# New orders, lags and banks for the five engines of a two-layer attention kernel, with known waits skipped

## The chip, the cores and the metric

The kernel runs on one core of one Trainium2 chip. A core has five engines that run their own queues of instructions in order: TensorE (PE, matrix products into PSUM), VectorE (DVE), ScalarE (ACT, functions from a table that must be loaded), GpSimd (POOL) and SyncE (SP, which here only issues transfers). They meet at semaphores. The metric is the device time of the program in microseconds (us). The measured kernel of before takes 1125.41 us, the median of 3 runs (1125.07 to 1126.71).

## The reference

64 sequences `x` of 64 tokens with 256 channels, and a context of the same shape. Layer 0 is cross attention, layer 1 a recurrent block (RWKV-like), all in fp32:

```python
h = concatenate([ctx, x]); q = x @ q_w + q_b; k, v = split(h @ kv_w + kv_b)       # 16 heads of 16
attn = softmax(where(mask, q @ k.T / 16, -inf)) @ v @ out_w + out_b + x
x = gelu(rmsnorm(attn) @ mlp_w1 + b1) @ mlp_w2 + b2 + x
xa = ln(x); sx = previous token of xa - xa
xxx = tanh((xa + sx * maa_x) @ maa_w1) @ maa_w2                                   # five mixes
xk, xw, xv, xr, xg = xa + sx * (maa_stack + xxx)
w = exp(-exp(time_decay + tanh(xw @ td_w1) @ td_w2)); r, k, v = xr @ Wr.T, xk @ Wk.T, xv @ Wv.T
g = silu(xg @ Wg.T)
for each token: out = r @ (u * k v + s); s = k v + w * s                          # 32 heads of 8
x1 = x + groupnorm(out) * g @ Wo.T
xc = ln(x1); x = x1 + sigmoid(xr2 @ Wfr.T) * (square(relu(xk2 @ Wfk.T)) @ Wfv.T)
```

## The kernel before

Channels lie on the 128 partitions in two halves; a group is 4 sequences (T = 256 tokens), and 16 groups are worked off. A group's work is cut into named pieces. What sets the order is a string for each engine, `PE_ORDER`, `ACT_ORDER`, `DVE_ORDER`, `POOL_ORDER` and `SP_ORDER` (lines 64 to 75). `turns` (line 86) walks each string once a turn; an entry `2:o` in turn i is piece `o` of group i - 2. The number is the lag. So up to five groups are in work at once, each engine goes through its own list in order, and an engine that waits holds up all that stands behind it. The planning was done outside the kernel; the code has only its result.

PSUM has eight banks. `BANK` (line 60) gives each product its bank, and `tenants` (line 93) works out who had the bank before. `filled[b]` and `freed[b]` count the fillings and readings of bank b: `ready` waits for a product, `taken` until a product was read. `opened` on PE (line 356) waits until the earlier tenant was read. `wait` waits for a value in SBUF.

The pieces of PE, in the order of a group's work: `q`, `k0`, `k1`, `v0`, `v1` (projections from `h_sb`); `sc0`, `sc1` (scores, banks `s0` to `s7`); `tr0` to `tr7` (transposed probabilities); `va0`, `va1`; `o`; `rms`; `w0` to `w3` and `c0` to `c3` (hidden layer up, `psum<-y`, and down, `psum<-hid`); `mean0`, `var0` (first layer norm, `psum<-hsum`); `maa` (`psum<-z`), `xp0`, `xp1`, `x4` (mixes, `psum<-th`); `td1`, `td2`; `K`, `V`, `R`, `G` (`psum<-xm`); `coef`; `ga0`, `ga1` (sums over the state, `psum<-rs`); `cen`, `gvar` (group norm); `O` (`psum<-og`); `mean1`, `var1` (second layer norm); `fk`, `fr` (`psum<-xf`); `fv` (`psum<-xc`, the squared relu).

Between them work, among others: on ACT `ex0` to `ex7` (exponentials of the scores, four instructions each), `pt`, `V`, `K`, `R` (copies from PSUM), `sq`, `lnr`, `lng`, `lna` (squares and inverse roots by Ln and Exp), `sh` (scale and shift), `th`, `tw` (Tanh), `ge0` to `ge3` (Gelu), `e1`, `decay`, `gu`, and the table loads `learnt` (Exp and Ln) and `squashed` (Tanh and Gelu); on DVE `mx` (row maxima), `in` (reciprocals), `y`, `x1`, `hm` and `hv` (sums `hsum` for the norms), `ct`, `nm`, `sx`, `z`, `tm` (`tmp`), `kv`, `st` (the recurrence, as a scan), `bonus`, `sum`, `gn`, `og`, `res`, `xf`; on POOL `pn` (normed probabilities), `xm`, `rk`, `rs` (state times receptance), `act`, `fin`. SP issues `h`, `mask`, `xa`, the small rows `row0` and `row1` (`st_sb`), `s0`, the output `store`, the weights (`load0`, `load1`), and `spread`: eight transfers `vb<-vr` that copy `V` to eight layouts for `kv`.

A matmul in fp32 leaves two records, so four matmuls read as x8.

Of the kernel before, what the change touches and what calls it, by code (L numbers as in the profile page):

```python
# [65 lines left out]
ACT_ORDER = """1:ev1 2:e1 2:decay 0:kt0 1:ysq 1:lna 2:row1 3:relu 2:squashed 2:G 3:tr 1:ge0 1:ge1 1:ge2 1:ge3 0:qt 1:sq0 1:learnt 1:lnr0 1:first 0:vv0 2:gsq 1:sh0
0:kt1 2:lng 0:row0 1:squashed 1:th 2:gu 0:learnt 0:ex1 0:vv1 0:ex0 0:ex2 1:squashed 1:tw 0:learnt 0:ex3 1:V 0:ex4 0:ex5 0:pt1 0:ex6 0:pt3 2:sq1 0:ex7
1:R 0:ev0 1:K 2:lnr1 0:pt5 0:pt7 2:sh1"""
DVE_ORDER = """1:mx3 1:in2 1:mx4 1:mx5 1:in3 1:pt0 1:pt2 1:in4 1:mx6 1:in5 1:mx7 2:tm4 1:in6 3:hv1 1:in7 1:pt4 1:at0 1:pt6 3:nm1 3:sx1 1:fold0 1:at1 3:xf0 2:kv0
2:kv1 2:st0 1:y 0:mask 1:ysum 3:xf1 2:kv2 2:kv3 1:yn 2:kv4 2:st1 2:kv5 2:gate 2:st2 2:kv6 2:st3 2:st4 2:st5 2:st6 2:bonus 1:fold1 2:kv7 1:x1 1:hm0  # L70
2:st7 1:ct0 1:hv0 2:sum 1:fold2 1:nm0 1:sx0 1:z 0:mx0 3:fin 2:gn 0:mx1 2:og 0:mx2 1:tm0 1:tm1 2:res 1:tm2 2:hm1 0:in0 1:tm3 0:in1 2:ct1"""
# [995 lines left out]
```

## Time and profile before

| | us |
|---|---|
| median of 3 runs | 1125.41 |
| the profiled execution | 1126.65 |
| its span, first to last instruction | 1124.9 |
| up to the first `w0` | 48.28 |
| first `w0` to second | 61.19 |
| second `w0` (109.47) to last (1004.69), fourteen turns | 895.22 |
| from the last `w0` on | 120.21 |

| engine | busy, share of the span |
|---|---|
| PE | 1011.7 us, 90% |
| DVE | 761.6 us, 68% |
| ACT | 720.2 us, 64% |
| POOL | 469.5 us, 42% |

The profile is one execution. A row of the view in order of time has the start, the length, the engine, the line of the kernel, the operation, what it writes and reads, and in brackets how long the engine had stood idle and what ended that. Rows whose lengths overlap are pipelined: what a piece costs PE is the distance from its start to the next start.

### The profile page before, as it was taken

Reading aid. Unit: us, or ns where it says so; the run is one execution under the profiler, and the core shown is the slowest. Engines: PE = TensorE matmul, PEld = TensorE weight load, DVE = VectorE, ACT = ScalarE, POOL = GpSimd, SP = SyncE. Lnnn points to the kernel's source line nnn. Section 1 sums busy time; section 2 is a strip of 40 time slices with the busy share of each in tenths; the row PEclk is TensorE's granted clock in tenths of the full one; section 3 lists DMA queues with packets and bytes.
Section 4 is the critical chain, followed back from the end, with each engine's and each line's share of the span. In section 5 each row is a group of like instructions: output and inputs, shape, how many; then the busy total and the mean of one; then the engine's idle time right before and its main releaser. Section 6 shows DMA issues by size and latency. Waiting matters only on the chain.

```text
span 1124.9 us, 20426 instructions
## 1 busy us (share of the span) xinstructions
PE 1011.7 (90%) x6760; PEld 746.6 (66%) x6760; DVE 761.6 (68%) x1275; ACT 720.2 (64%) x2008; POOL 469.5 (42%) x391
## 2 busy tenths in 40 slices
PE   5779999999999999999999999999999999997634
PEld 3566677676867768676867768686777767674412
DVE  2445677676867678686767678686767868685452
ACT  5466584948767594957758494866759494863322
POOL 1114354534435354434435354443535453444240
PEclk9898999999999999999999999999999999998866
DMA  8015060421515051331506042151505133050500
GB/s 293 1 35 76 1 104 8 76 44 45 76 33 87 1 95 26 61 59 45 76 18 103 1 82 38 48 73 44 76 1 104 17 70 51 20 76 10 75 10 9
DMA packets 37127, 61.02 MB, mean 54 GB/s; under 512 B 10464, under 2 KB 13088, under 8 KB 36896
## 3 DMA queue, kind: packets, MB, share of 16 engines
q1 hardware_dynamic: 37024, 59.72, 28.9%
q8 instruction: 56, 0.92, 0.3%
q14 instruction: 47, 0.39, 0.1%
HBM read 21.95 MB, written 4.19 MB: 23 GB/s over the span
## 4 chain that ended last, share of the span: by engine, by line
PE 71%; DVE 8%; SPq 7%; ACT 5%; issue 5%; DMA 3%; POOL 1%; DVEq 0%; POOLq 0%; ACTq 0%
PE psum L366 30%; PE psum L467 10%; SPq L322 6%; PE psum L391 5%; PE psum L384 4%; PE psum L429 4%; PE psum L415 3%; PE psum L498 3%; PE psum L538 3%; DMA st_sb<-stT 3%; PE psum L441 2%; DVE tmp L889 2%; ACT probs L612 2%; PE psum L371 2%; PE psum L548 2%
## 5 line engine op out<-in xcount | busy, mean ns | idle before, releaser
L981 POOL TENSOR_TENSOR rs<-st,rr 128x512 f32<-128x512 f32 x128 | 187.3, 1469 | 303.7 <-DVE st L911 257.0
L911 DVE TENSOR_TENSOR_SCAN st<-decay,kv 128x512 f32<-128x512 f32 x128 | 189.5, 1500 | 20.3 <-POOL rs L981 20.2
L612 ACT ACTIVATE probs<-psum,neg_max 128x128 f32<-128x128 f32 x512 | 183.1, 405 | 1.8 <-DVE neg_max L795 1.4
L956 POOL TENSOR_TENSOR probs<-probs,rsum 128x512 f32<-128x512 f32 x128 | 134.7, 1058 | 59.0 <-DVE rsum L800 59.0
L964 POOL TENSOR_TENSOR xm<-tmp,xs 128x512 f32<-128x512 f32 x80 | 93.6, 1180 | 124.8 <-DVE tmp L889 111.2
L366 PE MATMUL psum<-y,w_sb 128*128 128x256 f32 x512 | 120.2, 389 | 7.5 <-ACT xc L730 3.8
L612 ACT ACTIVATION_READ_ACCUMULATOR probs<-psum,neg_max 128x1 f32 x512 | 125.9, 246 | 0.0
L366 PE MATMUL psum<-xm,w_sb 128*128 128x256 f32 x512 | 124.9, 388 | 0.4 <-POOL xm L964 0.3
L467 PE MATMUL psum<-hid,w_sb 128*128 128x256 f32 x512 | 119.7, 382 | 0.0
L641 ACT ACTIVATE hid<-psum,vec 128x256 f32<-128x256 f32 x128 | 53.7, 471 | 101.5 <-PE psum L366 60.5
L366 PEld LDWEIGHTS psum<-y,w_sb 128*128 128x128 f32 x512 | 98.2, 194 | 26.2 <-DVE y L828 7.2
L467 PEld LDWEIGHTS psum<-hid,w_sb 128*128 128x128 f32 x512 | 96.0, 190 | 25.0 <-issue 12.6
L366 PEld LDWEIGHTS psum<-xm,w_sb 128*128 128x128 f32 x512 | 95.2, 193 | 16.8 <-POOL xm L964 4.5
L795 DVE TENSOR_REDUCE neg_max<-psum 128x4 f32<-128x512 f32 x128 | 85.4, 680 | 23.6 <-PE psum L419 23.6
L593 ACT ACTIVATE qt<-psum,q_bias,vec 128x256 f32<-128x256 f32 x64 | 30.9, 562 | 82.1 <-PE psum L366 82.1
L902 DVE TENSOR_TENSOR kv<-vb,kk 128x504 f32<-128x504 f32 x128 | 83.4, 673 | 0.0
L429 PE MATMUL psum<-mats,probs 128*128 128x128 f32 x512 | 75.6, 284 | 1.7 <-POOL probs L956 1.1
L366 PE MATMUL psum<-xf,w_sb 128*128 128x256 f32 x256 | 66.6, 407 | 11.0 <-DVE xf L747 10.9
L987 POOL TENSOR_TENSOR x<-x,sq 128x512 f32<-128x512 f32 x16 | 20.2, 1265 | 134.3 <-DVE sq L939 134.3
L429 PEld LDWEIGHTS psum<-mats,probs 128*128 128x128 f32 x512 | 59.9, 145 | 15.7 <-issue 5.8
L384 PE MATMUL psum<-h_sb,w_sb 128*128 128x512 f32 x128 | 62.4, 611 | 7.4 <-DMA h_sb<-hT 7.4
L391 PE MATMUL psum<-w_sb,h_sb 128*128 128x256 f32 x256 | 61.8, 384 | 6.1 <-DVE og L926 6.1
(120 smaller groups left out, 1838.2 us busy)
## 6 DMA issues: line engine op xcount, KB each, us to landing
vb<-vr SPq DMA_DIRECT2D x128, 256.0 KB, 7.4
h_sb<-hT SPq DMA_DIRECT2D x16, 512.0 KB, 3.7
xa_sb<-xT SPq DMA_DIRECT2D x16, 256.0 KB, 3.9
out<-x SPq DMA_DIRECT2D x16, 256.0 KB, 2.0
...
```

What stands on the lines that cost most here:

```text
L366: last = mm(to[:, n * T:(n + 1) * T], w(name, k, m * P, m * P + P), rhs[k], start=(k == 0), stop=(k == 1))
L384: last = mm(to, w("k", k, m * P, m * P + P), h_sb[:, k, :, :], start=(k == 0), stop=(k == 1))
L391: last = mm(to[:, i * C:(i + 1) * C], h_sb[:, k, 2 * n + i, :], w("v", k), start=(k == 0), stop=(k == 1))
L429: last = nc.tensor.transpose(to[:, n * P:(n + 1) * P], probs[:, u % PROBS, n, :], mat("ident"))
L467: last = mm(to[:, m * T:(m + 1) * T], w2_sb[:, 2 * n + i, m * P:(m + 1) * P], hid[:, n % 2, i, :], start=(n == 0 and i == 0 and m == 0), s ...
L612: last = fn(probs[:, u % PROBS, n, :], bank(g, f"s{u}")[:, n * P:(n + 1) * P], ACT.Exp, bias=neg_max[:, u % PROBS, n:n + 1], accum_out=sum ...
L795: nc.vector.tensor_reduce(neg_max[:, u % PROBS, :], bank(g, f"s{u}").rearrange("p (n k) -> p n k", n=4), AX.X, ALU.max, negate=True).then_ ...
L902: tt(kv[:, j, :, 1:S], batches(vb[:, j, :])[:, :, 0:S - 1], batches(flat(kk))[:, :, 0:S - 1], ALU.mult).then_inc(kv_made.sem, 1)
L911: nc.vector.tensor_tensor_scan(st[:, n % 2, :], decay[:, :, :, :].rearrange("p h b s -> p (h b s)"), kv[:, j, :, :].rearrange("p b s -> p ...
L956: tt(probs[:, u % PROBS, :, :], probs[:, u % PROBS, :, :], rsum[:, u % PROBS, :].unsqueeze(2).broadcast_to([P, 4, KEYS]), ALU.mult).then_i ...
L964: tt(xm[:, k % XM, :, :].rearrange("p h (b s) -> p (h b) s", b=GB), tmp[:, k % TMP, :, :].rearrange("p h (b s) -> p (h b) s", b=GB), xs[0] ...
L981: tt(rs[:, (RH * g + n) % RS, :], st[:, n % 2, :], flat(rr), ALU.mult).then_inc(rs_made.sem, 1)
```

## The change

Every order string, the lags in them and the banks are replaced. The pieces of DVE, POOL and SP stay the same and move. On PE too, with lags 0 to 3 for 0 to 4. ACT gets one more `learnt` and one more `squashed` a turn, eight loads for six. `reach` now remembers for each engine the highest value it has waited for on a semaphore and leaves a wait out that this already covers. And the bank wait (`opened`) stands ahead of the wait for the data in every piece of PE.

```diff
@@ -57,20 +57,20 @@
-BANK = {"q": 4, "k0": 3, "k1": 6, "v0": 1, "v1": 4, "bias": 1, "s0": 5, "s1": 2, "s2": 0, "s3": 1, "t0": 4, "t1": 7, "t2": 0, "t3": 4, "a0": 4, "s4":
...
+BANK = {"q": 4, "k0": 5, "k1": 7, "v0": 4, "v1": 0, "bias": 3, "s0": 3, "s1": 1, "s2": 6, "s3": 0, "t0": 2, "t1": 0, "t2": 5, "t3": 4, "a0": 6, "s4":
...
-SP_ORDER = """2:xa 1:row0 1:load0 3:spread 3:row1 4:store 1:load1 0:h 1:s0 0:mask"""
...
+SP_ORDER = """2:load1 3:spread 4:store 1:load0 1:row0 1:xa 0:h 1:s0 2:row1 0:mask"""
...
@@ -271,22 +271,29 @@
+        known = {}
+
+        def reach(eng, name, sem, value):
+
+            if value > known.get((id(eng), name), 0):
+                known[id(eng), name] = value
+                eng.wait_ge(sem, value)
+
         def ready(eng, g, name):
 
             if g >= 0:
                 b, n = USE[g, name]
-                eng.wait_ge(filled[b], n + 1)
+                reach(eng, ("filled", b), filled[b], n + 1)
...
         def wait(eng, event, g, k):
 
-            if g * event.n + k > 0:
-                eng.wait_ge(event.sem, g * event.n + k)
+            reach(eng, event.name, event.sem, g * event.n + k)
...
-            def average(g, name, src):
-
-                return mm(opened(g, name)[:, 0:T], mat("mean256"), src[:, :], start=True, stop=True)
+            def average(g, name, src, made):
+
+                to = opened(g, name)
+                wait(pe, made, g, 1)
+                return mm(to[:, 0:T], mat("mean256"), src[:, :], start=True, stop=True)
...
-                    for name in ("q", "k0", "k1"):
+                    for name in ("k0", "q", "k1"):
...
                 elif piece in ("K", "V", "R", "G"):
                     n = "KVRG".index(piece) + 1
+                    to = opened(g, piece)
                     wait(pe, xm_made, g, n + 1)
```

What moves on PE between the end of the hidden layer and the mixes, before (`c3`, `q`, `fv`, `mean0`, `v0`, `ga1`, `var0`, `cen`, `k1`, `gvar`, `sc0`, `maa`):

```order
L467 MATMUL psum<-hid,w_sb 128x256 x4
L366 MATMUL psum<-h_sb,w_sb 128x256 x4
L366 MATMUL psum<-xc,w_sb 128x256 x4
L371 MATMUL psum<-hsum,mats 128x256
L391 MATMUL psum<-w_sb,h_sb 128x256 x4
L538 MATMUL psum<-rs,heads 32x512 x4
L371 MATMUL psum<-hsum,mats 128x256
L548 MATMUL psum<-gt,center 128x512
L384 MATMUL psum<-h_sb,w_sb 128x512 x2
L551 MATMUL psum<-kk,same 128x512
L415 MATMUL psum<-kt,qt 128x128 x16
```

The same place on PE after (`c2` and `c3`, `fk`, `mean0`, `coef`, `ga1`, `var0`, `fr`, `tr0`, `cen`, `fv`, `maa`):

```order
L476 MATMUL psum<-hid,w_sb 128x256 x8
L373 MATMUL psum<-xf,w_sb 128x256 x4
L380 MATMUL psum<-hsum,mats 128x256
L552 MATMUL psum<-z,bonus_w 128x256 x2
L546 MATMUL psum<-rs,heads 32x512 x4
L380 MATMUL psum<-hsum,mats 128x256
L373 MATMUL psum<-xf,w_sb 128x256 x4
L437 MATMUL psum<-mats,probs 128x128 x4
L557 MATMUL psum<-gt,center 128x512
L373 MATMUL psum<-xc,w_sb 128x256 x4
L492 MATMUL psum<-z,w_sb 128x256 x2
```

One product instead of two stands between `c3` and `mean0`, and more work than before between `ga1` and `cen`.

DVE from the recurrence up to `x1` (`L911` and `L924` are the scans `st`), before:

```order
L902 TENSOR_TENSOR kv<-vb,kk 128x8x63
L911 SCALAR_TENSOR_TENSOR st<-decay,kv 128x512
L902 TENSOR_TENSOR kv<-vb,kk 128x8x63
L894 SCALAR_TENSOR_TENSOR gate<-gt,psum 128x512
L911 SCALAR_TENSOR_TENSOR st<-decay,kv 128x512
L902 TENSOR_TENSOR kv<-vb,kk 128x8x63
L911 SCALAR_TENSOR_TENSOR st<-decay,kv 128x512 x4
L917 TENSOR_TENSOR gt<-psum,vr 128x512
L902 TENSOR_TENSOR kv<-vb,kk 128x8x63
L833 SCALAR_TENSOR_TENSOR x<-psum,vec,xa_sb 128x256 x2
L840 TENSOR_TENSOR hsum<-x 128x256
L911 SCALAR_TENSOR_TENSOR st<-decay,kv 128x512
```

DVE after, up to the same instruction:

```order
L924 SCALAR_TENSOR_TENSOR st<-decay,kv 128x512 x2
L808 TENSOR_REDUCE neg_max<-psum 128x4 x3
L915 TENSOR_TENSOR kv<-vb,kk 128x8x63 x2
L760 SCALAR_TENSOR_TENSOR xf<-sx,vec,xs 128x256 x2
L924 SCALAR_TENSOR_TENSOR st<-decay,kv 128x512
L760 SCALAR_TENSOR_TENSOR xf<-sx,vec,xs 128x256 x2
L924 SCALAR_TENSOR_TENSOR st<-decay,kv 128x512
L915 TENSOR_TENSOR kv<-vb,kk 128x8x63
L813 RECIPROCAL rsum<-sums 128x4
L907 SCALAR_TENSOR_TENSOR gate<-gt,psum 128x512
L924 SCALAR_TENSOR_TENSOR st<-decay,kv 128x512
L808 TENSOR_REDUCE neg_max<-psum 128x4
```

Behind these comes the last scan and then `x1`. All eight scans now stand ahead of `x1`, with four row maxima and both `xf` among them; before, the eighth followed `hm0`.

ACT around `tw`, after (before, a softmax tile stood ahead of `tw`, and `gu` and `lng` further up):

```order
L595 ACT_TABLE_LOAD
L585 ACTIVATE kk<-psum,vec 128x512
L587 ACTIVATE kk<-kk 128x512
L597 ACT_TABLE_LOAD
L695 ACTIVATE tw<-psum 128x128
L619 ACTIVATE vv<-psum 128x512
L595 ACT_TABLE_LOAD
L625 ACTIVATE probs,sums<-psum,neg_max 128x128 x4
L591 ACTIVATE vr<-psum 128x512
L738 ACTIVATE og<-og,gnv 128x256 x2
```

The load ahead of the group norm's root (`kk`) is the added `learnt`.

## Rows read from the trace of the kernel before

**Rows 1.** Busy time by stretch: us, then each engine, clock, DMA share, GB/s
```profile
0.00:48.28 48.28, 28.49 (x223) 20.05 (x223) 14.67 (x39) 25.52 (x87) 8.77 (x15) 0.89 0.49 171
48.28:109.47 61.19, 53.10 (x367) 41.01 (x367) 28.09 (x70) 36.90 (x111) 16.40 (x15) 0.92 0.31 51
493.05:556.58 63.53, 61.41 (x424) 45.67 (x423) 47.59 (x79) 44.24 (x126) 29.40 (x24) 1.00 0.30 54
1004.69:1124.90 120.21, 70.50 (x276) 46.42 (x276) 58.62 (x79) 38.83 (x62) 37.71 (x27) 0.78 0.14 25
```

**Rows 2.** PE in order of time, one steady turn: start, us, instruction, [idle before]
```profile
506.33 1.99 PE L467 MATMUL psum<-hid,w_sb 128*128 128x256 f32 x8
508.16 1.89 PE L366 MATMUL psum<-h_sb,w_sb 128*128 128x256 f32 x8
...
511.62 0.59 PE L371 MATMUL psum<-hsum,mats 128*128 128x256 f32 x2
...
514.86 0.70 PE L371 MATMUL psum<-hsum,mats 128*128 128x256 f32 x2
515.82 1.13 PE L548 MATMUL psum<-gt,center 128*128 128x512 f32 x2 [0.26 <-DVE gt L921]
...
519.76 1.17 PE L415 MATMUL psum<-kt,qt 32*128 32x128 f32 x32 [0.24 <-issue]
...
523.13 1.96 PE L391 MATMUL psum<-w_sb,h_sb 128*128 128x256 f32 x8 [0.47 <-DVE og L926]
...
530.51 0.70 PE L371 MATMUL psum<-hsum,mats 128*128 128x256 f32 x2 [0.78 <-DVE hsum L840]
531.55 1.17 PE L415 MATMUL psum<-kt,qt 32*128 32x128 f32 x32 [0.35 <-DVE tmp L889]
```

**Rows 3.** DVE in order of time; then one POOL row; then one page group
```profile
508.43 0.88 DVE L833 SCALAR_TENSOR_TENSOR x<-psum,vec,xa_sb 128x256 f32<-128x256 f32 x2 [1.37 <-PE psum L467]
509.41 1.28 DVE L840 TENSOR_TENSOR hsum<-x 128x256 f32<-128x256 f32 x1
...
519.56 0.88 DVE L747 SCALAR_TENSOR_TENSOR z<-sx,vec,xs 128x256 f32<-128x256 f32 x2
...
530.04 0.41 DVE L840 TENSOR_TENSOR hsum<-x 128x256 f32<-128x256 f32 x1
...
551.66 0.85 DVE L820 SCALAR_TENSOR_TENSOR y<-psum,o_bias,xa_sb 128x256 f32<-128x256 f32 x2
...
509.15 1.26 POOL L981 TENSOR_TENSOR rs<-st,rr 128x512 f32<-128x512 f32 x1
...
L795 DVE TENSOR_REDUCE neg_max<-psum 128x4 f32<-128x512 f32 x128 | 85.4, 680 | 23.6 <-PE psum L419 23.6
```

**Rows 4.** ACT in order of time, the same turn
```profile
523.23 1.08 ACT L725 ACTIVATE og<-og,gnv 128x256 f32<-128x256 f32 x2
...
532.01 1.28 ACT L582 ACT_TABLE_LOAD   x1
533.30 0.37 ACT L612 ACTIVATE probs<-psum,neg_max 128x128 f32<-128x128 f32 x1
...
544.69 1.06 ACT L578 ACTIVATE probs_t<-psum 128x512 f32<-128x512 f32 x2
...
548.20 0.83 ACT L687 ACTIVATE decay<-psum,vec 128x252 f32<-128x252 f32 x2
549.06 0.62 ACT L693 ACTIVATE decay<-decay 128x504 f32<-128x504 f32 x1
```

**Rows 5.** Waits: total, times, longest; then PE, DVE, ACT rows near the end
```profile
ACT xs L654 <- DMA st_sb<-stT: 13.6, 6, 8.4
...
1044.02 3.72 PE L366 MATMUL psum<-xm,w_sb 128*128 128x256 f32 x16 [0.34 <-POOL xm L964]
...
1069.41 0.69 DVE L894 SCALAR_TENSOR_TENSOR gate<-gt,psum 128x512 f32<-128x512 f32 x1 [2.96 <-ACT gt L713]
...
1105.20 1.28 ACT L572 ACT_TABLE_LOAD   x1 [1.89 <-PE psum L371]
```

More of the change, by code:

```diff
@@ L57 @@
 LEARNT, SQUASHED = "natural_log_exp_and_others", "gelu_apprx_tanh_and_others"
-BANK = {"q": 4, "k0": 3, "k1": 6, "v0": 1, "v1": 4, "bias": 1, "s0": 5, "s1": 2, "s2": 0, "s3": 1, "t0": 4, "t1": 7, "t2": 0, "t3": 4, "a0": 4, "s4":
[3 rows of a table removed]
-PE_ORDER = """2:o 3:G 4:fk 2:rms 4:fr 2:w0 2:w1 2:w2 2:c0 2:c1 2:w3 2:c2 3:ga0 2:c3 1:q 4:fv 2:mean0 1:v0 3:ga1 2:var0 3:cen 1:k1 3:gvar 1:sc0 2:maa 1:v1 2:xp0 3:O
-2:xp1 2:td1 3:mean1 1:sc1 2:V 1:tr0 1:tr1 1:tr2 2:K 1:tr3 1:bias 2:x4 1:tr4 2:R 1:va0 3:var1 1:tr5 1:tr6 1:tr7 0:k0 1:va1 2:td2 2:coef"""
@@ L66 @@
[L66 to L69, printed above, removed]
@@ new lines @@
+PE_ORDER = """1:tr3 1:tr2 2:K 3:O 2:x4 2:td2 1:va0 3:mean1 1:tr5 2:R 1:tr6 3:var1 1:tr4 1:tr7 0:q 1:va1 0:k0 1:o 0:k1 0:v0 1:rms 2:G 0:sc0 1:w0 1:w1 1:c0 1:w2 1:c1
+2:ga0 1:w3 1:c2 1:c3 3:fk 1:mean0 2:coef 2:ga1 0:bias 1:var0 3:fr 0:tr0 2:cen 3:fv 1:maa 2:gvar 1:xp0 1:xp1 0:v1 1:td1 0:sc1 1:V 0:tr1"""
+ACT_ORDER = """4:relu 2:sq0 2:lnr0 3:row1 2:sh0 3:gsq 4:squashed 4:tr 2:th 3:learnt 3:lng 2:squashed 2:tw 1:vv1 1:learnt 1:ex4 2:V 3:gu 1:ex5 1:pt1 1:pt3 2:K 1:ex6
+2:e1 1:ex7 3:sq1 1:ev0 2:decay 1:pt5 2:R 3:lnr1 1:pt7 1:ev1 0:qt 1:ysq 0:kt1 0:kt0 3:sh1 1:lna 0:vv0 1:squashed 1:ge0 2:G 1:ge1 0:learnt 0:ex0 0:ex2
@@ new lines @@
+1:squashed 1:ge2 1:row0 1:ge3 0:learnt 0:ex3 1:first 0:ex1"""
+DVE_ORDER = """1:mx7 1:pt2 3:res 3:hm1 1:in5 2:tm4 3:ct1 1:in6 1:in7 3:hv1 1:at0 1:pt6 1:pt4 3:nm1 2:kv0 2:kv1 1:at1 2:kv2 2:st0 2:st1 1:y 1:ysum 2:kv3 2:kv4 0:mask
+3:sx1 1:yn 2:st2 2:st3 0:mx0 0:mx1 0:mx2 2:kv5 2:kv6 3:xf0 2:st4 3:xf1 2:st5 1:fold1 2:kv7 0:in0 2:gate 1:fold2 2:st6 0:mx3 2:st7 1:x1 1:hm0 0:fold0
+1:ct0 2:bonus 1:hv0 2:sum 1:nm0 0:in1 0:pt0 1:sx0 1:z 3:fin 1:tm0 1:tm1 1:tm2 0:in2 0:in3 1:tm3 2:gn 0:mx4 0:mx5 0:in4 0:mx6 2:og"""
@@ L378, in piece_of @@
                 if piece == "q":
-                    project(opened(g, "q"), "q", [h_sb[:, k, :, S:KEYS] for k in range(HALVES)]).then_inc(filled_by(g, "q"), 1)
+                    project(to, "q", [h_sb[:, k, :, S:KEYS] for k in range(HALVES)]).then_inc(filled_by(g, "q"), 1)
                 elif piece in ("k0", "k1"):
                     m = int(piece[1])
-                    to = opened(g, piece)
                     for k in range(HALVES):
@@ L387, in piece_of @@
                     n = int(piece[1])
-                    to = opened(g, piece)
                     for i in range(2):
@@ L446, in piece_of @@
                         pe.wait_ge(ld_w[1].sem, 16)
+                    to = opened(g, "o")
                     for bp in range(2):
                         taken(pe, g, f"a{bp}")
-                    project(opened(g, "o"), "o", [attn[:, :, k, :] for k in range(HALVES)]).then_inc(filled_by(g, "o"), 1)
+                    project(to, "o", [attn[:, :, k, :] for k in range(HALVES)]).then_inc(filled_by(g, "o"), 1)
                 elif piece == "rms":
-                    wait(pe, ysum_made, g, 1)
-                    average(g, "rms", ysum).then_inc(filled_by(g, "rms"), 1)
+                    average(g, "rms", ysum, ysum_made).then_inc(filled_by(g, "rms"), 1)
                 elif piece in ("w0", "w1", "w2", "w3"):
@@ L456, in piece_of @@
                         pe.wait_ge(folded.sem, 4)
+                    to = opened(g, piece)
                     wait(pe, normed, g, 1)
-                    project(opened(g, piece), "w1", [y[:, k, :] for k in range(HALVES)], (2 * n, 2 * n + 1)).then_inc(filled_by(g, piece), 1)
+                    project(to, "w1", [y[:, k, :] for k in range(HALVES)], (2 * n, 2 * n + 1)).then_inc(filled_by(g, piece), 1)
                 elif piece in ("c0", "c1", "c2", "c3"):
@@ L481, in piece_of @@
                         pe.wait_ge(ld_small.sem, 80)
+                    to = opened(g, "maa")
                     wait(pe, z_made, g, 1)
-                    to = opened(g, "maa")
                     for k in range(HALVES):
@@ L491, in piece_of @@
                     pair = (0, 1) if piece == "xp0" else (2, 3)
+                    to = [opened(g, f"x{n}") for n in pair]
                     taken(pe, g, "maa")
-                    to = [opened(g, f"x{n}") for n in pair]
                     for m in range(HALVES):
@@ L517, in piece_of @@
                 elif piece == "td2":
+                    opened(g, "td2")
                     taken(pe, g, "td1")
-                    opened(g, "td2")
                     to = wide(g, "td2")
@@ L540, in piece_of @@
                 elif piece == "coef":
+                    to = opened(g, "coef")
                     wait(pe, rk_made, g, 1)
-                    to = opened(g, "coef")
                     for m in range(HALVES):
```

46 lines of the change are left out of this document (24 added, 22 removed), and 6 rows, old and new, of the table BANK.

## The prediction

> **What bounds the kernel now.** I read first the table of busy times by stretch [rows 1], cut where TensorE (PE) starts the first hidden-layer product `w0` of a group. Up to the first `w0` it takes 48.28 us, to the second 61.19, to the last one (1004.69) fourteen more turns, and 120.21 us are left then. The fourteen turns make 1004.69 - 109.47 = 895.22, 63.94 each. In the turn shown PE is busy 61.41 of 63.53 us at clock 1.00; VectorE (DVE) 47.59, ScalarE (ACT) 44.24, GpSimd (POOL) 29.40. So PE sets the turn, and only three things can give time: the 2.1 us in which it stands, the turns that are longer than this one, and the ends, where PE is busy 28.49 of 48.28 and 70.50 of 120.21 us.
>
> Second, PE in order of time [rows 2]. The idle time stands in brackets: 0.26 before the centering `cen`, 0.24 before the scores `sc0`, 0.47 before `v1`, 0.78 before `mean1`, 0.35 before `sc1`: 2.10 together, and these same five return in nearly every turn. 63.53 - 2.10 = 61.43 is the turn of this work with no wait in it.
>
> Third, who makes turns longer [rows 5]: ACT waited six times, 13.6 us in all, for the 4 KB load `st_sb`, once for 8.4. That is the load `row1`, which SP issues behind the eight `vb` transfers. The mean turn is 0.4 above the one shown.
>
> **The change, part by part.** Work per group is the same on PE, DVE and POOL: only orders, lags and banks move. ACT gets two more table loads a turn, eight for six.
>
> *Old waits.* `cen` gets `var0`, `fr` and `tr0` between itself and `ga1` (before only `var0`): gone. `sc0` waited for nothing but its eight semaphores; they are now four or five, the known ones being skipped: I take 0.1 left. `v1` opened a bank that `cen` held until DVE read it, and now takes bank 0 from `maa`, read by ACT before `xp0`: gone. `mean1` gets `x4`, `td2` and `va0` behind `O`, some 2.3 us against a chain of two DVE instructions: gone. `sc1` stood for `tmp`; it now stands 4.6 us behind the start of `xp0`, the third `tmp` is ready at some 4.4: gone, but close. The row load is issued before the spread of the next group and has most of a turn to land: the 0.4 goes.
>
> *New waits.* A product of four matmuls over 256 columns takes 1.73 (3.46 for `q` and `fv`, from 508.16 to 511.62) [rows 2]. Before, these two covered what lies between `c3` and `mean0`; now only `fk` does, 1.73. The chain there: `x1` 0.88, `hm0`, and about 0.1 for each hand-over. `hm0` took 1.28 where POOL worked beside it (POOL 509.15 for 1.26) and 0.41 where it did not [rows 3]. So `mean0` could follow `c3` by 1.5 or 2.4, and PE waits nothing or 0.7. POOL's `rs7` now starts as `x1` does, so nearer to the second. Also DVE can come late to `x1`. From `y` (551.66, or 488.1 a turn earlier) to where it stood ready for `x1` (508.43 - 1.37 idle = 507.1) it took 19.0. In that stretch the change puts `sx1`, four `mx`, the first `xf` and one reciprocal, takes out one `kv`, `bonus` and a wait of 1.3 for POOL: with 0.68 a `mx` [rows 3] some +1.6, plus about 1.2 in which it now waits for `ysq` and the root. With `y` starting 1.0 behind `o` that makes 22.8 from the end of `o`, against 22.2 of PE work (eight `w` and `c`, `k1`, `v0`, `G` at 1.73 make 19.0; `sc0`, `rms`, `ga0` and changes of shape 3.2). 0.6 late at most; I take 0.8 for `mean0` in all, 0 and 1.6 being the ends.
>
> `mean0` to `var0`: the chain `ct0`, `sq0`, `hv0` takes 2.7; the cover is `mean0`, `coef`, `ga1`, 2.4: 0.3. `var0` to `maa`: from 514.86 to the end of `z` (519.56 + 0.88) are 5.6 [rows 2, 3], the cover `var0`, `fr`, `tr0`, `cen`, `fv` makes 5.5: 0.1. For the many other hand-overs that now stand within half a microsecond (`K`, `td2`, `q`, `tr3`, `O`) I take 0.2 together, with 0.1 of `sc0` 0.3. New turn: 61.4 + 0.8 + 0.3 + 0.1 + 0.3 = 62.9.
>
> *ACT.* The longest run without rest is now from `tw` to `pt7`, before `va1` may start. The same run before went from the load at 532.01 to 545.75: 13.74. The change adds `gu` 1.08, `e1` 0.83 and `decay` 0.62 to it and takes one softmax tile, 1.4 (four instructions, spaced 0.35), out [rows 4]: 14.9. It starts 5.4 behind `xp0`, so `pt7` is done at 20.3; PE comes to `va1` 21.1 behind `xp0` by the same kind of count. Slack 0.8: no wait, but this is the place where the new order is tightest. Of the two added loads one stands before `lng`, the other beside the hidden layer (`learnt` and `squashed` around `ex0`, `ex2`), where ACT waits for PE. I cost both at nothing; uncovered they cost 1.28 each.
>
> A load takes 1.28, and the next instruction starts 0.01 behind it (532.01 + 1.28 = 533.29, then 533.30) [rows 4]. The Trainium skill, page "ScalarE: Activation LUTs", section "What ACT_TABLE_LOAD costs", gives 1283 ns for the load, as here, and a drain of 1380 ns more at every switch to another set; that page asks to group work by set, which speaks against eight loads. By the rows two loads more are 2.6 us of ACT a turn, by the page 5.3. It is the slower rival below.
>
> *First turns.* The order opens with `q`, `k0`, `k1`, `v0` and `sc0` of group 0, and now puts five pieces of group 1 before the first `w0`, into idle time. The softmax of group 0 still sets that point: 48.3, 47 to 53. The load of the later weights is issued behind `h` of group 1, some 20 us later, yet first needed after 48. To the second `w0` I count 57 instead of 61.2: 61.4 less `O`, `mean1`, `var1`, `ga0`, `gvar` of groups that do not exist yet and less part of the ACT run; the third is 62.
>
> *The end.* From the last `w0` to `V` of that group (1044.02) it took 39.3 [rows 5]. In the new order some 33: the hidden layer and `ga0` 14.9 with their changes of shape, then 2.5, 2.7, 5.7 by the chains above, 2.5 from `maa` to `xp0` and 4.6 to `V`. -6. Then DVE stood 2.96 for `gt`, because ACT stood 8.4 for the row [rows 5]: -3. The last `lnr1` (1105.20) loads two tables on the chain, since no `learnt` piece is left there; now one stands ahead of `lng` in the same turn: -1.3 there and two of 1.28 at `lnr1`: -3.9. Against these, `kv0` of the last group waits a little longer behind `nm1`, and scans and POOL hold each other up as before: I take back 3. 120.2 - 10 = 110, from 106 to 116.
>
> **Sum.** 48.3 + 57 + 62 + 13 x 62.9 + 110 = 1095.0 for the span. The profiled execution took 1126.65 at a span of 1124.9, 1.75 more, and the median of the runs is 1125.41, 1.24 below it: 1095.0 + 1.75 - 1.24 = 1095.5, say 1096.
>
> **Rivals.**
> *A, forecast*, turn 62.9: 1096.
> *B, all covered.* `hm0` takes 0.41, DVE is in time, PE waits 0.3: turn 61.8, 1096 - 13 x 1.1 = 1082. For it: each new wait was rounded up. Against: `rs7` beside `hm0`.
> *C, a turn no shorter than the one shown.* DVE comes 1.5 or more late to `x1`, or two of the near hand-overs fall on the other side; turn 63.7 to 64.2, 13 x 1.0 more: 1109, faster by the ends alone. For it: DVE and POOL slow each other by amounts that depend on how they meet.
> *D, slower: the ACT run is the bound.* Between `maa` and `K` it now holds three table loads. If each costs as long again as its row, 3 x 1.3 = 3.9, less the slack of 0.8, PE waits 3.1 a turn more: 1096 + 13 x 3.1 = 1136. It decides against the change from 29 / 13 = 2.3 us a turn on, when the run is 3.1 longer than I count. Against it: the 0.01 behind every load in [rows 4]. The page's rule on the drain is this case; the trace does not bear it out.
> *E, nothing to be seen* from skipped waits and banks, and gains at the ends given back in the turns: 1125.
>
> **Numbers.** A 0.50, B 0.13, C 0.24, D 0.09, E 0.04. Predicted is A, 1096. The range takes in B and C and the width of the ends: 1078 to 1117. A measurement of this kernel tells 0.2%, 2.3 us, from no change. Faster 0.87, same 0.03, slower 0.10.
>
> **What would show it.** Turns from `w0` to `w0` of 62.9; the five old waits gone; in their place `mean0` waiting for `hsum` by under 1 us and `var0` by some 0.3; ACT never waiting for `st_sb`; `va1` not waiting for ACT; the last `w0` near 985 and 110 us behind it; no pair of table loads in the last `lnr1`. The forecast is wrong if the turn is above 64, or if PE waits for ACT at `K`, `va1` or `q` in each turn.

## The result, and the profile after

The changed kernel takes 1078.15 us (median of 4 runs, 1072.45 to 1079.97), the kernel before, on the same chip, 1126.06 (4 runs, 1125.07 to 1127.48): ratio 0.957, interval 0.955 to 0.959. The forecast was 1096 with a range of 1078 to 1117. The direction was right and the size was not: 48 us gained where 29 were forecast.

Busy time by stretch, the changed kernel, cut again at the starts of the first, second and third `w0`, around one steady turn and at the last `w0`; the answer to [rows 1]. Columns: stretch, us, then PE, PEld, DVE, ACT, POOL, clock, DMA share, GB/s.

```profile
0.00:54.57 54.57, 37.33 (x279) 26.91 (x279) 14.96 (x37) 29.40 (x93) 8.78 (x15) 0.87 0.48 152
54.57:114.68 60.11, 51.53 (x366) 39.19 (x362) 32.55 (x73) 39.47 (x113) 18.71 (x16) 0.89 0.32 52
...
479.09:539.61 60.52, 59.41 (x426) 44.96 (x422) 46.15 (x79) 46.73 (x127) 31.27 (x24) 1.00 0.32 56
...
962.62:1076.80 114.18, 68.38 (x297) 48.16 (x295) 60.05 (x81) 41.50 (x66) 37.53 (x26) 0.81 0.15 26
```

The third stretch, to 176.43, is 61.75. So the first `w0` stands at 54.6 (48.3 forecast), the next two stretches are 60.1 and 61.75 (57, 62), thirteen turns average (962.62 - 176.43) / 13 = 60.48 (62.9), and the end is 114.2 (110). The turns were forecast 31.5 us too long in all, the ends and the second stretch 13.6 too short. The turn is where the miss is. It lost 2.00 us of busy PE (61.41 to 59.41), where the prediction had it unchanged, and stands for 1.1 us in place of 2.1.

PE in the same turn in order of time, the answer to [rows 2]; idle time before a row in brackets.

```profile
494.20 1.89 PE L373 MATMUL psum<-xf,w_sb 128*128 128x256 f32 x8
496.09 0.67 PE L380 MATMUL psum<-hsum,mats 128*128 128x256 f32 x2
...
498.90 0.67 PE L380 MATMUL psum<-hsum,mats 128*128 128x256 f32 x2 [0.28 <-DVE hsum L866]
...
501.57 1.02 PE L557 MATMUL psum<-gt,center 128*128 128x512 f32 x2
...
506.96 1.16 PE L505 MATMUL psum<-th,maa_sb 32*128 32x256 f32 x16
508.05 1.99 PE L399 MATMUL psum<-w_sb,h_sb 128*128 128x256 f32 x8
510.44 0.66 PE L522 MATMUL psum<-xm,w_sb 128*64 128x128 f32 x8 [0.40 <-POOL xm L977]
511.36 1.17 PE L423 MATMUL psum<-kt,qt 32*128 32x128 f32 x32 [0.25 <-DVE tmp L902]
...
512.82 1.97 PE L373 MATMUL psum<-xm,w_sb 128*128 128x256 f32 x8 [0.17 <-POOL xm L977]
```

The waits ahead of `cen`, `v1` and `mean1` are gone and that of `sc0` does not show. `mean0` (496.09) follows `fk` with no idle time shown; the only new wait that the prediction named and that shows is `var0`'s 0.28. `td1` 0.40, `sc1` 0.25 and `V` 0.17 wait behind `xp0`/`xp1`. The sixteen products of `xp0` and `xp1` now make one group of 1.16 us, and `v1` starts 1.09 behind them. This is the main thing that the prediction missed.

DVE in the same turn, the answer to [rows 3], and then the scans as a group of the page.

```profile
477.88 2.33 DVE L924 TENSOR_TENSOR_SCAN st<-decay,kv 128x512 f32<-128x512 f32 x2
...
494.40 0.88 DVE L846 SCALAR_TENSOR_TENSOR x<-psum,vec,xa_sb 128x256 f32<-128x256 f32 x2 [1.03 <-PE psum L476]
495.31 0.64 DVE L853 TENSOR_TENSOR hsum<-x 128x256 f32<-128x256 f32 x1
...
L924 DVE TENSOR_TENSOR_SCAN st<-decay,kv 128x512 f32<-128x512 f32 x128 | 163.6, 1301 | 0.5 <-POOL rs L994 0.5
```

DVE is not late to `x1`: it stands 1.03 us for PE. `hm0` took 0.64, between the 0.41 and 1.28 of [rows 3]. A scan takes 1301 ns on average, as against 1500 before.

ACT, the answer to [rows 4]: three loads of 1.28 (one ahead of `kk`, one on either side of `tw`), then the last transposed tile and the wait behind it.

```profile
506.58 1.28 ACT L595 ACT_TABLE_LOAD   x1
...
509.24 1.28 ACT L597 ACT_TABLE_LOAD   x1
511.15 0.28 ACT L695 ACTIVATE tw<-psum 128x128 f32<-128x128 f32 x1 [0.62 <-PE psum L522]
...
511.93 1.28 ACT L595 ACT_TABLE_LOAD   x1
...
526.52 0.60 ACT L591 ACTIVATE probs_t<-psum 128x512 f32<-128x512 f32 x1
529.36 0.48 ACT L636 ACTIVATE o_even<-psum,vec 128x256 f32<-128x256 f32 x1 [2.23 <-PE psum L449]
```

`pt7` ends at 527.12, 20.2 behind `xp0`; PE starts `va1` at 528.15, 21.2 behind it. The prediction had 20.3 and 21.1. This count was right.

The end, the answer to [rows 5]: ACT of the last two groups, with the loads that stand on its way, then PE at `V` of the last group.

```profile
981.42 1.28 ACT L585 ACT_TABLE_LOAD   x1
983.29 1.28 ACT L587 ACT_TABLE_LOAD   x1
...
1010.47 1.28 ACT L585 ACT_TABLE_LOAD   x1
1012.26 1.28 ACT L587 ACT_TABLE_LOAD   x1
...
1059.88 0.47 ACT L585 ACTIVATE r_rs<-psum,vec 128x256 f32<-128x256 f32 x1 [1.77 <-PE psum L380]
...
997.26 3.32 PE L373 MATMUL psum<-xm,w_sb 128*128 128x256 f32 x7 [1.70 <-POOL xm L977]
```

The wait for `st_sb` is gone, and the last `lnr1` (1059.88) has no load. But the code issues the pieces `learnt` and `squashed` only for groups that exist, so now the two `lnr` before it have two loads each on their way, at 981 and at 1010. `V` of the last group starts 34.6 behind the last `w0` (33 forecast).

### The profile page after: what moved, and what is told of

Read it like the earlier page. It is cut to its first block, busy times and chain, and to the rows that moved or that the text cites. A ratio compares the mean times of both kernels' runs of the same rounds, so it can differ in the third digit from the quotient of the medians.

```text
span 1076.8 us, 18987 instructions
## 1 busy us (share of the span) xinstructions
PE 979.2 (91%) x6760; PEld 735.7 (68%) x6760; DVE 753.3 (70%) x1275; ACT 762.3 (71%) x2040; POOL 500.2 (46%) x391
## 4 chain that ended last, share of the span: by engine, by line
PE 80%; DVE 6%; ACT 5%; POOL 5%; issue 4%; DMA 0%; POOLq 0%; DVEq 0%; SPq 0%; ACTq 0%
PE psum L373 36%; PE psum L476 10%; PE psum L393 5%; PE psum L437 5%; PE psum L380 4%; POOL xm L977 4%; PE psum L399 3%; PE psum L449 3%; PE psum L492 2%; PE psum L423 2%; PE psum L505 2%; PE psum L546 1%; PE psum L561 1%; ACT probs L625 1%; PE psum L552 1%
## 5 line engine op out<-in xcount | busy, mean ns | idle before, releaser
L994 POOL TENSOR_TENSOR rs<-st,rr 128x512 f32<-128x512 f32 x128 | 206.5, 1629 | 226.6 <-DVE st L924 196.7
L969 POOL TENSOR_TENSOR probs<-probs,rsum 128x512 f32<-128x512 f32 x128 | 146.7, 1157 | 181.6 <-DVE rsum L813 181.6
L924 DVE TENSOR_TENSOR_SCAN st<-decay,kv 128x512 f32<-128x512 f32 x128 | 163.6, 1301 | 0.5 <-POOL rs L994 0.5
L625 ACT ACTIVATION_READ_ACCUMULATOR probs<-psum,neg_max 128x1 f32 x512 | 116.5, 228 | 0.0
L373 PEld LDWEIGHTS psum<-y,w_sb 128*128 128x128 f32 x512 | 94.8, 190 | 27.4 <-issue 15.8
L915 DVE TENSOR_TENSOR kv<-vb,kk 128x504 f32<-128x504 f32 x128 | 96.3, 781 | 0.0
L902 DVE SCALAR_TENSOR_TENSOR tmp<-psum,vec,sx 128x256 f32<-128x256 f32 x128 | 54.6, 479 | 53.8 <-PE psum L505 42.8
L808 DVE TENSOR_REDUCE neg_max<-psum 128x4 f32<-128x512 f32 x128 | 82.2, 675 | 13.4 <-PE psum L427 13.4
L595 ACT ACT_TABLE_LOAD x64 | 82.1, 1283 | 1.1
L597 ACT ACT_TABLE_LOAD x64 | 82.1, 1283 | 1.1
L437 PE MATMUL psum<-mats,probs 128*128 128x128 f32 x512 | 71.3, 279 | 2.5 <-POOL probs L969 1.3
L399 PE MATMUL psum<-w_sb,h_sb 128*128 128x256 f32 x256 | 65.7, 402 | 2.1 <-ACT probs L625 2.1
```

Source lines behind the costliest of these rows:

```text
L373: last = mm(to[:, n * T:(n + 1) * T], w(name, k, m * P, m * P + P), rhs[k], start=(k == 0), stop=(k == 1))
L399: last = mm(to[:, i * C:(i + 1) * C], h_sb[:, k, 2 * n + i, :], w("v", k), start=(k == 0), stop=(k == 1))
L437: last = nc.tensor.transpose(to[:, n * P:(n + 1) * P], probs[:, u % PROBS, n, :], mat("ident"))
L595: sc.preload_act_table_set(LEARNT)
L625: last = fn(probs[:, u % PROBS, n, :], bank(g, f"s{u}")[:, n * P:(n + 1) * P], ACT.Exp, bias=neg_max[:, u % PROBS, n:n + 1], accum_out=sum ...
L808: nc.vector.tensor_reduce(neg_max[:, u % PROBS, :], bank(g, f"s{u}").rearrange("p (n k) -> p n k", n=4), AX.X, ALU.max, negate=True).then_ ...
```

## The experiments

All are one edit to one of the two kernels. "Turn" is the median from `w0` to `w0` in the profiled execution, between the third `w0` and the fifteenth; medians of times are of several runs. Against the changed kernel only the turns tell small differences: its own runs lie between 1072.45 and 1079.97. The "fill" is the stretch up to the first `w0`, the "end" that from the last one on.

**1. `v1` between `xp0` and `xp1`.**

```
-2:gvar 1:xp0 1:xp1 0:v1 1:td1
+2:gvar 1:xp0 0:v1 1:xp1 1:td1
```

> The changed kernel with xp1 moved behind v1, nothing else. In the changed kernel xp0 and xp1 together take 1.09 us of TensorE, before each took 1.06. Theory 1: the four mixes use four different 32-row strips of the array, and their products run beside each other only when they are adjacent in the queue. Then both take 1.06 again here, TensorE is busy 1.0 longer in a turn, and the waits of 0.40, 0.26 and 0.17 behind them mostly go, because they only stand there since the mixes are early: turn 60.5 to 60.8, the time 1078 to 1083. Theory 2: the 1.09 is an artefact of missing or modelled records; then the start distances from xp0 to td1 stay and the turn stays 60.5.

Measured: 1089.61 us (1082.54 to 1092.77). The turn is 61.24, PE busy 60.38. The rows on PE:

```profile
505.03 1.13 PE L505 MATMUL psum<-th,maa_sb 32*128 32x256 f32 x8
506.09 1.99 PE L399 MATMUL psum<-w_sb,h_sb 128*128 128x256 f32 x8
508.02 1.13 PE L505 MATMUL psum<-th,maa_sb 32*128 32x256 f32 x8
509.08 0.66 PE L522 MATMUL psum<-xm,w_sb 128*64 128x128 f32 x8
```

Here `td1` (509.08) waits for nothing. Each half takes 1.06 when it stands alone and both together take 1.09: the four strips of 32 rows run beside each other. Standing together saves 0.97 of busy time a turn; 0.25 of it goes back into waits. Net 0.72, 13 turns of which are 9.4 us. So the first theory had the cause right, and turn and time came out above what it expected, since fewer waits went away than it took.

**2. Every wait issued again.**

```
-            if value > known.get((id(eng), name), 0):
-                known[id(eng), name] = value
+            if value > 0:
                 eng.wait_ge(sem, value)
```

> The changed kernel with every wait issued again, known or not (1912 waits on TensorE for 1321), orders, lags and banks as changed. Theory A: a wait that is already met costs TensorE about 0.05 us where pieces are short, so the transposes take 0.50 instead of 0.44 each and the turn grows by 0.6 to 1.0 us, the time by 10 to 16. Theory B: met waits are passed ahead of time and cost nothing except in front of the scores (0.24 once a turn): turn grows by 0.1 to 0.3, the time by 2 to 5.

Measured: 1085.44 (1084.84 to 1091.08), turn 60.87, PE busy 59.58. PE issues 1912 waits in the program in place of 1321, 37 more a group, and a turn is 0.35 longer, half of it in PE's busy time and half in its waits. Neither number expected (0.6 to 1.0, or 0.1 to 0.3) held. Shared out over PE's 37, that is some 0.01 us for a wait already met, as an estimate, for the edit brings waits back on the other engines too. The end is 118.7 in this execution for 114.2; what makes it longer stays open.

**3. The new code with the old tables of orders and banks.**

```
-BANK = {...}  PE_ORDER ... SP_ORDER of the changed kernel
+BANK = {...}  PE_ORDER ... SP_ORDER of the kernel before
```

> The kernel before in orders, lags and banks, with the new code: known waits skipped (1354 for 1831 on TensorE) and bank waits first. Theory A: 0.6 to 1.0 us a turn less, 1110 to 1116. Theory B: 0.1 to 0.3 less, 1121 to 1125, and all else of the gain is in the tables.

Measured: 1119.68 (1116.17 to 1127.3), turn 63.38, PE busy 61.12. The median lies between the two expectations, nearer to B. The ratio to before is 0.996 (0.994 to 0.999). So of the 48 us the code (known waits skipped, bank waits first) gives some 6 by the medians, 1 to 7 by the interval, and the tables 41. The turn of before was 63.70 in the median: 0.3 from the code, 2.9 from the tables.

**4. Data waited for first, banks after** (the body of the TensorE block of before, with the new tables and skipped waits; one of some twenty such places).

```
-                    to = opened(g, piece)
                     wait(pe, normed, g, 1)
-                    project(to, "w1", ...
+                    project(opened(g, piece), "w1", ...
```

> The changed kernel with the waits of each piece of TensorE in the old order (data first, bank second), known waits still skipped. Both theories: bank waits are nearly always met, so which stands first matters little: 1078 to 1080. A theory by which bank waits first is worth something (the last wait in the queue is the one that is late) gives 0.05 at each of the four places that wait, 0.2 a turn, 1081.

Measured: 1072.97 (1068.48 to 1077.55), turn 60.33, where `var0` waits 0.19 in place of 0.28. In the new order "bank waits first" costs 0.19 a turn, 2.5 us in all; the times alone do not show it, they lie within the scatter of the changed kernel.

**5. The row load `row1` of before, issued ahead of `spread`.**

```
-SP_ORDER = """2:xa 1:row0 1:load0 3:spread 3:row1 4:store ...
+SP_ORDER = """2:xa 1:row0 1:load0 3:row1 3:spread 4:store ...
```

> The kernel before with one edit: on SP's queue the store that fills scratch rows for the second norm stands ahead of the transfer that spreads gamma, instead of behind it. Theory: in before, three of 15 turns ran 3 to 6 us late only because ScalarE or SP's queue waited there, and part of the end's 110 us is the same wait; with the order exchanged no turn is longer than 64.2 and the time falls by 4 to 9 us, to 1116 to 1121. Rival: the time is set by TensorE's own instructions and the five waits, so nothing moves: 1124 to 1127.

Measured: 1122.22 (1117.43 to 1125.99), ratio to before 0.997 (0.9945 to 0.9991). ScalarE waits for `st_sb` nowhere in it. In the kernel before, four of the six such waits reached PE: `w0` opens the bank of `fk`, and ScalarE's `relu`, which reads it, stands behind `row1`. First ScalarE and PE in order of time, then PE's line in the view of waits (total, times, longest), all of the kernel before:

```profile
237.22 0.21 ACT L654 ACTIVATE xs<-st_sb 128x8 f32<-128x8 f32 x1 [1.65 <-DMA st_sb<-stT]
...
238.06 4.12 PE L366 MATMUL psum<-y,w_sb 128*128 128x256 f32 x18 [1.68 <-ACT xc L730]
...
PE psum L366 <- ACT xc L730: 3.8, 4, 1.7
```

These 3.8 us are gone. From the second `w0` to the last it takes 893.1 in place of 895.2, so 2.2 less: this execution has two turns of 65.06 where the other has one of 65.05. In such a turn PE is busy 62.94 and not 61.4, and the granted clock is at the lower level for 3.4 us; the stretch in the kernel before, in the columns of [rows 1]:

```profile
723.70:727.10 3.40, 3.40 (x40) 2.72 (x38) 2.34 (x6) 3.03 (x10) 3.40 (x4) 0.50 0.00 0
```

Why the clock fell in these turns and not in others, which have the same waits ahead of that point, stays open. 4.0 more are in the end (116.1 for 120.2), where the wait of 8.4 us is gone, and 1.6 are lost again between the first `w0` and the second. So the theory was right on the waits, and wrong that no turn would be longer than 64.2.

**6. The first `v1` in bank 7.**

```
-            bank = BANK[name]
+            bank = 7 if (g, name) == (0, "v1") else BANK[name]
```

> The changed kernel with the very first v1 (group 0) put in bank 7 in place of bank 0, where it waited for the scores of the first group to be read (2.09 us on ScalarE's probs) before 16 matmuls at half clock. Theory that this wait is on the path of the fill: first w0 starts 2 us earlier (52.5 where the changed kernel had 54.6) and the time is 1075 to 1077. Rival, that the fill is set by ScalarE's own work: first w0 stays at 54 to 55 and the time at 1078 to 1079.

Measured: 1071.83 (1071.08 to 1073.95), first `w0` at 50.13, the next stretch 58.1. The fill's PE rows, first of the changed kernel, then of this one:

```profile
25.07 3.78 PE L399 MATMUL psum<-w_sb,h_sb 128*128 128x256 f32 x8 [2.09 <-ACT probs L625]
```

```profile
22.66 3.57 PE L399 MATMUL psum<-w_sb,h_sb 128*128 128x256 f32 x8
27.20 1.17 PE L423 MATMUL psum<-kt,qt 32*128 32x128 f32 x32 [0.97 <-DVE probs_t L818]
```

The wait of 2.09 is gone and half of it comes back ahead of `sc1`, now for DVE. In both, `v1` takes about twice its 1.89 us; PE had been idle for most of the 5 us ahead (busy 1.65 between 20 and 25 in the changed kernel), and the granted clock of the changed kernel between 25 and 30 us is 0.50, the lower level (1.2 GHz). The first `w0` came 4.4 us sooner than in the profiled execution of the changed kernel, more than the 2 expected. Most of that is no effect of the edit: a second execution without it, in the next experiment, has 50.94.

**7. The same table asked for twice more.**

```
-1:vv1 1:learnt 1:ex4
+1:vv1 1:learnt 1:learnt 1:learnt 1:ex4
```

> The changed kernel with two more table loads in each turn, right behind the learnt one that stands ahead of ex4 (ten loads a turn in place of eight). A traced load takes 1.28 us, so 2.57 us more of ScalarE a turn; the last transposed probabilities are ready 1.0 us ahead of va1. Theory A (a load costs its 1.28 us and nothing else, slack 1.0): turn 60.5 to 61.5 or 62.0, time 1093 to 1102. Rival B (each switch also costs a drain of 1.38 us that the row does not show): turn + 4.3, time 1140 to 1150. Rival C (ScalarE has more slack there than the last wait shows): turn below 60.9, time under 1085.

Measured: 1074.87 (1072.41 to 1079.06), turn 60.53, and still 64 rows of loads for each of the two pieces: the added requests for a table that is already in left no row and took no time. Whether the chip passes over them or they never reach it, the run does not show, and it says nothing on ScalarE's slack. It is of use as a second execution of the changed kernel: its first `w0` stands at 50.94 where the one above has 54.57, its third stretch is 60.30 for 61.75, its turns are equal to 0.01 us. By the third `w0` the two executions stand 6.6 us apart (176.43, 169.87), by which products of the fill meet the lower clock: `k0` and `k1` of group 0 took 4.66 us there and 3.60 here, three tiles of probabilities 2.79 and 2.17, the second `q` 3.35 and 1.89. A single profiled execution tells the fill to some 4 us and a steady turn to 0.01. Over the ten executions that have the new tables the first `w0` stands between 50.1 and 54.6, over the four with the old ones between 48.3 and 48.8.

**8. Table loads kept in the last two turns.**

```
-            if 0 <= i - lag < GROUPS and ...
+            if (0 <= i - lag < GROUPS or piece in ("learnt", "squashed") and GROUPS <= i - lag and i <= GROUPS + 1) and ...
```

> The changed kernel with the table loads named learnt and squashed also issued in the two turns behind the last group, where the changed kernel leaves them out because the group that they belong to does not exist. Without them six loads of the end stand exposed in front of the work that needs them (two in front of each of the pairs at 981 and 1010 us, one at 1045 and one hidden at 1069). Theory: each load taken off the chain that ends last gives 1.28 us, three to four of them are on it: 1073 to 1075, the stretch from the last w0 to the end 109 to 110 in place of 114.2. Rival: the end is set by TensorE's recurrence and VectorE, the loads only moved the idle time: 1077 to 1079, stretch 113 to 114.

Measured: 1074.24 (1069.1 to 1074.93). ScalarE at the end:

```profile
974.29 0.63 ACT L662 ACTIVATE sq<-xc 128x512 f32<-128x512 f32 x1 [0.62 <-DVE xc L861]
976.32 0.47 ACT L585 ACTIVATE r_rs<-psum,vec 128x256 f32<-128x256 f32 x1 [1.40 <-PE psum L380]
...
1000.70 0.63 ACT L662 ACTIVATE sq<-xc 128x512 f32<-128x512 f32 x1 [0.75 <-DVE xc L861]
...
1004.77 1.09 ACT L684 ACTIVATE xs<-xc,vec 128x256 f32<-128x256 f32 x2 [1.21 <-DVE xc L870]
```

No load stands between `sq` and the `lnr` behind it (976.32), and from the second `sq` to the `xs` two steps behind (1000.70 to 1004.77) it is 4.1 us, where it was 6.3 (1008.46 to 1014.79). The end is 111.2 long, against 114.2 and 114.4 in the two executions without the edit: 3.1 us, 2.4 loads' worth, where three to four were expected.

**9. A maximum between two scans.**

```
-2:st2 2:st3 0:mx0
+2:st2 0:mx0 2:st3
```

> The changed kernel with one maximum (mx0) put between the scans st2 and st3 on VectorE, which stand next to each other in it. In the changed kernel two scans that stand together take 2.33 us; in the kernel before single ones took 1.70 us each, beside work of GpSimd. Theory A (a scan is short because another scan follows it): the two now take 1.5 to 1.7 each, VectorE is busy 0.7 us longer in a turn, x1 has 1.03 us in hand, so the turn stays at 60.5 and the time within the run to run scatter of the changed kernel (1072 to 1080). Theory B (they are short because GpSimd is not at work at that moment): they stay at 1.17 each.

Measured (one run): 1081.32, turn 60.70. DVE, then the GpSimd product that meets the second scan:

```profile
478.75 1.22 DVE L924 TENSOR_TENSOR_SCAN st<-decay,kv 128x512 f32<-128x512 f32 x1
...
480.65 1.74 DVE L924 TENSOR_TENSOR_SCAN st<-decay,kv 128x512 f32<-128x512 f32 x1
...
480.04 1.27 POOL L994 TENSOR_TENSOR rs<-st,rr 128x512 f32<-128x512 f32 x1 [4.22 <-DVE st L924]
```

Neither expectation held as put: the first scan stayed at 1.22, the second went to 1.74. It starts while GpSimd's `rs` is at work (480.04 to 481.31). In the changed kernel the second one of the pair starts just before `rs` does (479.0 and 479.18) and takes 1.2. That is a pattern of these rows and not a proof of its cause. DVE still stands 0.85 us ahead of `x1`, so the 0.5 us themselves did not reach PE. The turn is 0.18 longer all the same, as a wait of 0.18 ahead of `mean0`: `hm0` went from 0.64 to 0.82 us, and `mean0` follows it. GpSimd's last `rs` ends 0.54 us into `hm0` here and 0.36 into it in the changed kernel, which is the likely reason and was not tested. DVE's time in hand at `x1` is no slack of `mean0`.

**10. `xp0` and `xp1` together in the kernel before.**

```
-2:maa 1:v1 2:xp0 3:O 2:xp1 2:td1
+2:maa 1:v1 2:xp0 2:xp1 3:O 2:td1
```

> The kernel before with one edit: xp0 and xp1 stand next to each other in TensorE's order, O behind them. Theory, that K=32 products on four row strips run beside each other when nothing stands between them (1.16 us for both in the changed kernel, 1.06 for each in the kernel before): TensorE's busy time of a turn falls from 61.41 to 60.4, a part of it turns into waits (td1 now has more time, mean1 less), so the turn falls by 0.5 to 1.1 us and the time by 7 to 16 us, to 1109 to 1118. Rival, that the other new orders make it and not these two: 1124 to 1127.

Measured: 1186.79 (1180.97 to 1190.44), 5% slower than before. PE in one turn:

```profile
552.88 1.13 PE L498 MATMUL psum<-th,maa_sb 32*128 32x256 f32 x8
555.58 1.81 PE L498 MATMUL psum<-th,maa_sb 32*128 32x256 f32 x8 [1.56 <-ACT vv L606]
557.32 3.78 PE L366 MATMUL psum<-og,w_sb 128*128 128x256 f32 x8
```

`xp1` opens bank 4, which `v1` had just filled, and ScalarE copies that bank only behind an exponential. The wait of 1.56 separates the two halves again, and behind it the granted clock falls from 0.99 (552 to 556) to 0.50 (556 to 566), the lower level of 1.2 GHz, so that `O` takes 3.78 us and not 1.99. This turn is 69.2 us with 65.7 busy; the median one is 68.2. The same wait stands in every turn, but in three of the twelve the clock stays at 1.00:

```profile
420.56 1.13 PE L498 MATMUL psum<-th,maa_sb 32*128 32x256 f32 x8 [1.56 <-ACT vv L606]
421.62 1.99 PE L366 MATMUL psum<-og,w_sb 128*128 128x256 f32 x8
```

That turn is 66.0 with 61.7 busy. So about 2.3 us a turn are lost in waits at the full clock, and 3.1 more in a turn like the first of these two at the lower one, which does not follow each time. The order alone loses here; that it would gain with a free bank for `xp1` was not tried in the kernel before.

**11. Two more loads that change the table.**

```
-1:vv1 1:learnt 1:ex4
+1:vv1 1:learnt 1:squashed 1:learnt 1:ex4
```

> The changed kernel with the squashed table and then the learnt table loaded once more in each turn behind the load that stands ahead of ex4, so that both added loads change the table (two loads of the table already there left no row in the run before this one). 2.57 us more of ScalarE in each turn. The last transposed probabilities are ready 1.0 us ahead of va1, and ScalarE waits 0.45 us ahead of ex4. Theory A (a load costs its traced 1.28 us, slack 1.0 to 1.5): turn 61.5 to 62.2, time 1088 to 1100. Rival B (a switch costs 2.66 us, 1.38 of it in no row): turn + 3.5 or more, time over 1125. Rival C (the order leaves ScalarE more slack): turn under 61.0, time under 1085.

Measured: 1110.58 (1110.31 to 1111.12), turn 62.58. ACT, then PE in that turn:

```profile
527.11 1.28 ACT L595 ACT_TABLE_LOAD   x1
528.40 1.28 ACT L597 ACT_TABLE_LOAD   x1
529.69 1.28 ACT L595 ACT_TABLE_LOAD   x1
...
532.54 1.99 PE L373 MATMUL psum<-xm,w_sb 128*128 128x256 f32 x8 [1.27 <-ACT probs L625]
```

2.57 us more of ScalarE make the turn 2.06 longer: the slack was 0.5 us, not 0.8, and it ended not at `va1` but at `K`, whose bank held scores that the exponentials were still reading. The loads stand 1.29 apart, and ScalarE's next instruction (530.98) starts 0.01 behind the third. The Trainium skill gives 2.66 us for a switch, 1283 ns for the load and 1380 for a drain (page "ScalarE: Activation LUTs", section "What ACT_TABLE_LOAD costs"). Two switches would be 5.3 us by it; a rise of 2.06 and rows without a gap do not bear out the drain. The 1283 ns for the load alone are borne out.

**12. Edits 4, 6 and 8 together** in the changed kernel.

> The changed kernel with three edits that each gave something: TensorE waits for its data first and for its bank after (0.19 us a turn), the first v1 in bank 7 (about 1 us in the first 110), and the table loads learnt and squashed kept in turns 16 and 17 (3.1 us at the end). If they add up: turn 60.33, first w0 at 49 to 51, end 111, time 1066 to 1069. If they overlap: 1069 to 1073.

Measured: 1066.19 (1065.93 to 1067.17), ratio to before 0.947 (0.945 to 0.948), turn 60.32, first `w0` at 50.80, end 110.4. The turn has what experiment 4 gave (0.2), the end what experiment 8 gave and 0.8 more. The edit of the fill does not show: the third `w0` stands at 170.5, where the execution of experiment 7 had 169.9 without it. By the medians this version is 12 us below the changed kernel, and 9 below the same program in experiment 7; 6 of them lie in the turns and the end, the rest in the fill, which scatters by 4.

## Why the prediction was right or wrong

**What bounds the kernel:** right. PE is busy 59.41 of 60.52 us. ScalarE is not far behind: it had 0.5 us in hand (the eleventh experiment).

**Work per group is the same on PE:** this step failed. The instructions are the same, their time is not. PE busy fell by 2.00 a turn. The groups of one turn, by line (busy us, mean ns), before and after:

```profile
L429 PE MATMUL psum<-mats,probs 128*128 128x128 f32 x32 | 4.6, 277 | 0.0
...
L498 PE MATMUL psum<-th,maa_sb 32*128 32x256 f32 x16 | 2.3, 400 | 0.0
```

```profile
L437 PE MATMUL psum<-mats,probs 128*128 128x128 f32 x32 | 4.3, 273 | 0.0
...
L505 PE MATMUL psum<-th,maa_sb 32*128 32x256 f32 x16 | 1.2, 400 | 0.0
```

1.1 of the 2.0 is `xp0` and `xp1` standing together, which the first experiment showed (0.97); 0.17 is the skipped waits (the second). 0.3 is the transposes: 0.1 of it shows with the old tables in the new code too (the third), the second did not bring it back, and its cause is open. The rest is about a tenth less or more in single pieces (`cen`, `coef` and `O` less, `gvar` more), and no run separated it. The base of the turn was 61.4 in the sum and 59.4 on the chip: 26 us over 13 turns. The sign to be read ahead of time was in the trace of before. The mean of one product was 400 ns, sixteen of them make 6.4 us, and the group's busy time was 2.3; the products of such a group already ran beside each other, so what stood next to the group mattered. The Trainium skill says of different tiles of the array that they can work in parallel (page "TensorEngine Tiling (Array Packing)", section "Key Properties"); these rows agree.

**Old waits:** right for `cen`, `sc0`, `v1` and `mean1`; `sc1`, called close, still waits 0.25. Of the 2.1, 1.85 went. The row load was right too: of the 0.4 by which the mean turn was longer than the one shown, 0.27 were its waits and 0.1 one stretch at the lower clock (the fifth experiment).

**`mean0`, 0.8:** mis-sized; it cost 0.16. No idle time shows ahead of it, but it starts 1.89 behind `fk`, which takes 1.73 to the next start elsewhere, and 0.14 behind the end of `hm0` (495.95), as it does in the ninth experiment. DVE was forecast 0.6 late to `x1` and was 1.03 early. From `y` (472.58) to that point (493.37) it took 20.8 us; 21.8 were forecast. Six scans stand in between, each 0.2 us shorter on average (1301 for 1500 ns), and were left at their old time. So `mean0` has no slack: the ninth experiment put 0.18 more there with one `mx` moved.

**`var0` 0.3:** right, 0.28; 0.09 of it is the bank wait put first (0.19 without). **The 0.3 for hand-overs** went to `td1` (0.40) and `V` (0.17) instead: since `xp1` starts a microsecond sooner, GpSimd's `xm` comes late for them; with `v1` back between the halves neither waits. Idle time is 1.1 in all, 1.5 forecast.

**ACT run:** the count to `pt7` and `va1` was right within 0.1. That this is where the order is tightest was wrong: `K`'s bank comes first, with 0.5 in hand. Rival D needed 1.3 us for each of three loads beyond its row. The eleventh experiment found none.

**First turns, 48.3 and 57:** 54.6 and 60.1 in the profiled execution, 50.9 and 58.6 in another of the same program. The range of 47 to 53 for the first `w0` held one of the two. The step that failed is that the added pieces run in idle time. `v1` of group 0 waits 2.09 for a bank and takes twice its time at the lower clock; with another bank for it the first `w0` stood at 50.1, so that is about 1 us. The rest lies in the pieces of group 1: from 44.14 to 54.57 PE stands only 0.61. How much each costs was not separated.

**The end, 110:** 114.2. The step that failed is the loads: they were counted off the last `lnr1` (-3.9, and that pair did go), and the two pairs that the same rule puts ahead of the two `lnr` before it were not looked for. Kept loads make it 111.2; the last 1.2 above the forecast were not traced to a cause.

**Rivals.** B, all covered, had the time (1082) nearest to 1078, but by luck: its turn of 61.8 was 1.3 too long and its first turns and end too short. C, D and E did not come.
